# Rotary attention: PV of four query tiles issued in two portions of four key tiles instead of four portions of two

## The reference, cut to what matters

```python
q = jnp.concatenate([q[:, :, :1, :], _rope(q[:, :, 1:, :])], axis=2)
k = jnp.concatenate([k[:, :, :1, :], _rope(k[:, :, 1:, :])], axis=2)
dots = jnp.einsum('bhqd,bhkd->bhqk', q, k) * SCALE
attn = jax.nn.softmax(dots, axis=-1)
out = jnp.einsum('bhqk,bhkd->bhqd', attn, v)
out = out.transpose(0, 2, 1, 3).reshape(B, N, NUM_HEADS * DIM_HEAD)
return out @ w_out
```

## Time and profile before

| | |
|---|---|
| median of 3 runs | 1670.22 us |
| the three runs | 1657.77, 1670.22, 2057.99 us |
| the profiled execution | 1668.52 us |
| its span, first to last instruction | 1666.5 us |
| mean granted TensorE clock over the span | 0.845 |

### The profile page before, as it was taken

How to read it: one execution, slowest core, us unless ns; L and a number is a source line. 1 busy time by engine, 2 the same in 40 slices (tenths; PEclk the granted TensorE clock), 3 DMA queues, 4 the chain that set the end, 5 groups by cost and what they waited for, 6 DMA issues and landing times. The chain is left out here.

```text
span 1666.5 us, 26411 instructions
## 1 busy us (share of the span) xinstructions
PE 1471.6 (88%) x9399; PEld 959.6 (58%) x9400; DVE 833.4 (50%) x1461; ACT 900.2 (54%) x1582; POOL 281.1 (17%) x206
## 2 busy tenths in 40 slices
PE   3599999999999999999999982691889999999995
PEld 2376667666666766766666662461555555555443
DVE  5355445445544554455455443353685555554506
ACT  2267667666767767677677651230534444444443
POOL 3233123113312321231133112103100000000000
PEclk9799999999999999999999995795865557665557
DMA  4442244234234423433342335112000000000001
GB/s 139 110 108 73 66 105 107 51 97 108 69 76 105 106 55 80 107 90 71 90 107 69 76 95 177 43 47 57 1 1 1 1 1 1 1 1 1 1 1 31
DMA packets 53495, 105.22 MB, mean 63 GB/s; under 512 B 9010, under 2 KB 30004, under 8 KB 53300
## 3 DMA queue, kind: packets, MB, share of 16 engines
q1 hardware_dynamic: 52004, 100.59, 24.4%
q0 software_dynamic: 1424, 3.67, 0.8%
HBM read 18.70 MB, written 5.31 MB: 14 GB/s over the span
## 5 line engine op out<-in xcount | busy, mean ns | idle before, releaser
L505 DVE TENSOR_REDUCE a_negmax<-a_score 128x1 f32<-128x1024 f32 x257 | 314.8, 1225 | 406.5 <-PE a_score L371 406.5
L466 ACT ACTIVATE a_probs_T<-a_tr 128x512 f32<-128x512 f32 x514 | 279.2, 594 | 256.2 <-PE a_tr L377 256.2
L472 ACT ACTIVATE a_probs<-a_score,a_negmax 128x1024 f32<-128x1024 f32 x256 | 286.4, 1119 | 28.7 <-DVE a_negmax L505 28.6
L430 PE MATMUL a_out<-a_probs_T,a_v 128*64 128x256 f32 x2088 | 283.0, 392 | 0.6 <-DVE a_attn_T L521 0.6
L377 PE MATMUL a_tr<-ident,a_probs 128*128 128x128 f32 x2056 | 267.4, 273 | 0.0
L377 PEld LDWEIGHTS a_tr<-ident,a_probs 128*128 128x128 f32 x2056 | 240.7, 140 | 35.5 <-issue 0.6
L1298 DVE TENSOR_REDUCE a_lowest<-a_score 128x1 f32<-128x512 f32 (+3 forms) x320 | 183.7, 631 | 129.0 <-PE a_score L1174 76.6
L1266 ACT ACTIVATE a_probs_T<-a_score_T 128x1024 f32<-128x1024 f32 (+1 forms) x192 | 149.2, 810 | 168.0 <-PE a_score_T L1154 149.6
L430 PEld LDWEIGHTS a_out<-a_probs_T,a_v 128*64 128x64 f32 x2088 | 126.8, 136 | 116.5 <-issue 66.9
L1171 PE MATMUL a_score<-a_k_all,a_q_all 32*128 32x512 f32 (+3 forms) x384 | 162.4, 599 | 6.6 <-DVE a_lowest L1298 6.4
L331 POOL TENSOR_TENSOR a_rden<-a_rden_col,a_ones 128x256 f32<-128x256 f32 x65 | 68.4, 1052 | 574.8 <-DVE a_rden_col L528 574.8
(11 more groups left out here) (235 smaller groups left out, 2161.5 us busy)
## 6 DMA issues: line engine op xcount, KB each, us to landing
a_q_rot<-a_q_raw SPq DMA_DIRECT2D x68, 128.0 KB, 2.3
a_k_rot<-a_k_raw SPq DMA_DIRECT2D x68, 128.0 KB, 2.3
a_xn_cur<-normed_T SPq DMA_DIRECT2D x17, 512.0 KB, 3.2
a_k_stack0ah<-a_k_hi SPq DMA_DIRECT2D x18, 256.0 KB, 3.3
a_k_stack0al<-a_k_lo SPq DMA_DIRECT2D x18, 256.0 KB, 4.7
a_k_stack0bh<-a_k_hi SPq DMA_DIRECT2D x18, 256.0 KB, 5.0
a_k_stack0bl<-a_k_lo SPq DMA_DIRECT2D x18, 256.0 KB, 4.7
a_k_stack1ah<-a_k_hi SPq DMA_DIRECT2D x16, 256.0 KB, 3.3
```

The lines of the kernel that those rows point to most:

```text
L430: ins = nc.tensor.matmul(out_ps[64 * h:64 * h + 64, 0:256], v[par if s >= 5 else 1 - par][:, k, 64 * h:64 * h + 64], probs_T[grp][:, h, k, ...
L466: nc.scalar.activation(probs_T[(s - 1) // 4 % 2][:, h, 4 * i:4 * i + 4, tile % 2 * P:tile % 2 * P + P], tr_ps[i][:].rearrange("p (k q) -> ...
L472: nc.scalar.activation(probs[s % 4][:], score_ps[s % 2][:], ACT.Exp, bias=negmax[:, s:s + 1], accum_out=den[:, s:s + 1]).then_inc(probs_re ...
L505: nc.vector.tensor_reduce(negmax[:, s:s + 1], score_ps[s % 2][:], axis=AX.X, op=ALU.max, negate=True)\
```

## The change

The four portions of two key tiles become two portions of four. A portion is issued in the even slots only (r = 1 and r = 3: slots 2, 6, 10, 14 and 4, 8, 12, 0); the odd slots issue none. The wait for `attn_ready` and for the copies of the transposes moves with the first portion from slots 1, 5, 9, 13 to slots 2, 6, 10, 14, and the denominators' transposes in those slots wait for `attn_ready` too. Ahead of the loop two portions on zeroed operands become one of four key tiles.

```diff
                         elif s % 4 == 2:
                             pe.wait_ge(rden_ready, at(4, s // 4 + 1))
+                            pe.wait_ge(attn_ready, at(4, s // 4 + 1))
                             for q in range(2):
...
                         r, grp = (s - 5) % 4, (s - 5) // 4 % 2
-                        if r == 0:
+                        if r == 1:
                             for i in range(2):
-                                pe.wait_ge(tr_copied[i], at(SLOTS, s))
-                            pe.wait_ge(attn_ready, at(4, s // 4 + 1))
-                            if s == 5:
+                                pe.wait_ge(tr_copied[i], at(SLOTS, s - 1))
+                            pe.wait_ge(attn_ready, at(4, (s - 1) // 4 + 1))
+                            if s == 6:
                                 pe.wait_ge(misc_free, at(ITEMS, 0))
-                        for k in (2 * r, 2 * r + 1):
-                            for h in range(2):
-                                ins = nc.tensor.matmul(out_ps[64 * h:64 * h + 64, 0:256],
-                                                       v[par if s >= 5 else 1 - par][:, k, 64 * h:64 * h + 64],
-                                                       probs_T[grp][:, h, k, :], start=k == 0, stop=k == TB - 1)
+                        if r % 2 == 1:
+                            for k in range(2 * r - 2, 2 * r + 2):
+                                for h in range(2):
+                                    ins = nc.tensor.matmul(out_ps[64 * h:64 * h + 64, 0:256],
+                                                           v[par if s >= 5 else 1 - par][:, k, 64 * h:64 * h + 64],
+                                                           probs_T[grp][:, h, k, :], start=k == 0, stop=k == TB - 1)
                         if r == 3:
                             ins.then_inc(pv_done, 1)
...
                 for h in range(2):
-                    for k in range(6):
+                    for k in range(4):
                         nc.tensor.matmul(out_ps[64 * h:64 * h + 64, 0:256], v[1][:, k, 64 * h:64 * h + 64],
```

## The result

| | before | after |
|---|---|---|
| median | 1666.06 us (4 runs: 1657.77, 1661.90, 1670.22, 2057.99) | 1615.77 us (4 runs, 1614.09 to 1619.23) |
| profiled execution | 1668.52 us | 1619.23 us |
| span | 1666.5 us | 1617.3 us |

The ratio of after to before is 0.972, with a 95% interval of 0.967 to 0.977: 2.8% faster. It leaves out the run of 2057.99 us, a slow one; without it the median of before is 1661.90. Forecast were 1622 us, with 1608 to 1645 as the range.

The account below looks back on a forecast made before the run. TensorE's sequence was taken to bound the attention, with a DMA chain deciding from slot 10 to slot 15. First pair -1.8, 15 pairs -45.2, tail +0.3: -46.7 us on 1668.5, giving 1622 us, range 1608 to 1645.

Parts of the forecast that it names:

- TensorE's sequence is the time: In the attention, TensorE's own sequence sets the time apart from few waits; busy 678.3 of 696.0 us.
- A border costs 0.34 us, in and out: Going into and out of a PV portion on TensorE loses 0.34 us; 8 of 16 are removed per pair.
- The pair is TensorE up to slot 10 and a chain of 17.1 us behind it: TensorE decides slot 15 to slot 10, then the k_stack chain; 3.01 us saved a pair, 0.74 of wait left.
- The first pair -1.8 us: First pair of heads, up to its slot 10, gains 5 x 0.34 + 0.10 = 1.8 us.
- The tail +0.3 us: Behind the last slot 15, later PV work set against one border saved costs 0.3 us.
- Slot 14's transposes up to 0.2 us late, under the wait: After short slot 13, ScalarE's copies may delay slot 14's transposes up to 0.2 us, covered by the k_stack wait.
- The chances: Faster by over 2% 0.74, same 0.20, slower 0.06.
- half of the rest: Half of the 0.06 chance given to something between the forecast and the rivals, counted towards "same".
- Rival A: Way out of PV belongs to the scores, so a border removed gives only 0.14 us: -26 us, 1642; chance 0.13.
- Rival B: Odd slots without PV wait for ScalarE's copies or exponentials; at full size +51 us, 1720; chance 0.05.
- Rival C: Odd slots of scores and transposes drop TensorE's clock to half, 1.6 us a pair: 25 us, 1647; chance 0.06.

Follow-up runs that it names:

- the two kernels without a wait: VectorE's cast of k moved from slot 10 to slot 9, in the kernel before and the changed kernel: 56.07 and 53.42 us a pair, 1660.31 and 1602.72 us.
- The full-width runs: PV matmuls using all 128 columns, in the kernel before and the changed kernel: 64.39 and 64.45 us a pair, 1786.49 and 1783.40 us.
- one portion of eight: Changed kernel with PV as eight key tiles in slots 4, 8, 12, 0: 1657.15 us; cast in slot 9, 1601.90 us; plus split k_stack wait, 1593.02 us.
- the repeat: Both kernels profiled again without an edit: before 1660.23 us (8 runs), changed 1614.69 us (4 runs), ratio 0.969 against 19 further runs of before.

## Why the prediction was right, step by step

- **TensorE's sequence is the time**: right. It went from 57.23 to 54.28 us a pair with the same matmuls.
- **A border costs 0.34 us, in and out**: right, 0.331 by the two kernels without a wait. The full-width runs show that it goes with the 128*64 tiling, for which the forecast had only the place of the loss.
- **The pair is TensorE up to slot 10 and a chain of 17.1 us behind it**: right. The sum gave 3.01 us a pair and 0.74 us of wait; measured were 2.95 and 0.80 (mean of 0.82 and 0.78; the sign named for it, 0.5 to 0.75 us, was a little low). In the changed kernel the next slot 15 was released at 498.55, 17.1 us after slot 10's first score at 481.44. The same split foretold that one portion of eight would be slower, and that removing the wait would give 0.8 us a pair (it gave 0.86).
- **The first pair -1.8 us**: in the profile -0.9, since TensorE's clock stayed at half until 68.1 us instead of 66.5. In the second profile of the changed kernel the clock rose at 66.3, and the first pair took 1.9 us less than in the first profile of before.
- **The tail +0.3 us**: +0.1, from 20.79 to 20.88 us between the last slot 15 and the next layer's first matmul.
- **Slot 14's transposes up to 0.2 us late, under the wait**: 0.07 late (494.22 to 494.52 is 0.30), and slot 12 took 3.85 us, as forecast. Slot 13 took 1.82, a little under the 1.9 to 2.1 named as the sign, since the score behind its transposes begins early.
- **Missed, without harm to the total**: the sum was made against an execution that contained two disturbed turns, and I read their waits in the earlier trace rows as part of the kernel that stays. Against this profile the difference was -49.2, of which 7.7 are these turns; against the second profile of before the attention ended 45.5 us earlier (997.65 and 952.16), beside the 46.7 forecast. The medians differ by 46.1 without the run of 2057.99 us (50.3 with it), and in the repeat by 45.5 against the 8 runs and by 49.0 against the 19. The forecast lies among them, and closer than some 3 us the runs can't tell. The 1622 stand 6 us above the measured median because they were counted down from an execution 6.6 us above the 1661.90.
- **The chances**: A, C and half of the rest are 0.13 + 0.06 + 0.03 = 0.22, where the text has 0.20 for "same"; it decides nothing.
- **Rival A**: would have made a pair 1.71 us shorter; it fell by 2.95. It falls by the 53.42 us and by the row at 500.81, too. The sign that I had named for it, first scores of about 0.33 behind an item, is there all the same, but the score starts early by as much. Starts alone mislead; the distance from the item to the second score does not.
- **Rival B**: its place was right, its size not. ScalarE's lateness is 0.07 us in one slot; only with one portion of eight does it grow, to 0.3 us a pair.
- **Rival C**: in the changed kernel the clock stays at full in the loop. One portion of eight was the harder test: with three slots in a row of scores and transposes the granted clock was 1.00 over 700 us as long as no long wait came. By the rule of the Trainium skill named there (TensorE: Matmul & The Clock Gate, Part 4: PE-mode transpose) transposes do not count as busy for the clock; this stream, where they are mixed with scores, does not show it.

## What to carry to other kernels

Look for the borders between tilings in a stream of matmuls, price one from the distances of starts, and gather the matmuls of one tiling. Then ask what releases the loop: here the borders saved in front of the DMA chain paid in full, while one portion of eight moved still more PV in front of the chain, and lost until the chain was started earlier. Look at the distances of all turns of a loop before making a sum against one profile.

## What was not expected of the hardware

- A turn of the loop can begin with TensorE idle for 0.7 to 3.1 us while instructions are fetched again, 9 packets more for each such turn; the view names another releaser or none. It came in four of fourteen profiles, with 41 to 95 packets in the instruction queue, and never with 32. All four have a loop with 16 places of PV in a pair (of six such profiles), none the eight profiles with 8 or 4. The number of TensorE's instructions in a turn is the same, about 1607, so what decides it stays open.
- Behind waits of 2.7 to 3.0 us once a pair the granted clock fell to half in nine of 15 pairs, about 1.6 us each. Length alone doesn't decide it: the wait of 2.91 us in the row at 404.09 was followed by full clock, one of 2.74 by half. It fell behind three of the nine stalls of 1.8 to 2.2 us and behind the one of 3.1; behind waits of 0.7 to 1.3 us it never did in the loop.
- Two PV matmuls on the column halves run side by side: their records start some 7 ns apart, and the next two 0.216 us later (0.866 for the eight records of a portion), while at full width each record takes 0.216.
